# A linear attention and FP4 feed-forward block: Silu on ScalarE, tiles of two sequences, and x's rounding moved to VectorE

## The reference

```python
xn = layernorm(x)
# attention: 16 heads of 16 values, buckets of 64 tokens
q = softmax(q over the head's 16 values) * 0.25;  k = exp(k)
context[n] = sum over all buckets before n of  k_bucket^T v_bucket     # and the sums of k
attn = (q @ context) / max(q @ ksum, 1e-6);  branch1 = attn @ W_out.T
# feed-forward with fp4 quantise-dequantise of every operand, in blocks of 16
h = silu(fp4(xn) @ fp4(w_gate).T) * (fp4(xn) @ fp4(w_up).T)             # 704 wide
branch2 = fp4(h) @ fp4(w_down).T
out = x + branch1 + branch2
```

## Time and profile before

| | before |
|---|---|
| median of three runs | 1790.64 us (1788.91 to 1790.73) |
| the profiled execution's own time | 1790.21 us |
| its span, first to last instruction | 1788.5 us |
| DVE busy | 1723.7 us (96%) |
| PE busy | 1677.6 us (94%) |
| ACT busy | 1142.6 us (64%) |
| POOL busy | 599.4 us (34%) |
| DMA | 21 GB/s, 6.7% of 16 engines |

### The profile page before, as it was taken

One profiled execution on the slowest core, in us unless ns is written; L12 is line 12 of the kernel. 1 busy time (PEld: TensorE's weight loads), 2 busy tenths in 40 slices (PEclk: granted clock), 3 DMA queues, 4 the chain that ended last, 5 costly groups with the idle time before them and its releaser, 6 DMA issues.

```text
span 1788.5 us, 47623 instructions
## 1 busy us (share of the span) xinstructions
PE 1677.6 (94%) x12366; PEld 1147.8 (64%) x12366; DVE 1723.7 (96%) x4655; ACT 1142.6 (64%) x2840; POOL 599.4 (34%) x1053
## 2 busy tenths in 40 slices
PE   0289999999999999999999999999999999999997
PEld 0256666666666666666666666666666666666665
DVE  6769999999999999999999999999999999999997
ACT  2756666666666666666666666666666666666663
POOL 2723232333333333333333333333333333333330
PEclk9889999999999999999999999999999999999998
DMA  3000000000000000000000000000000000000000
GB/s 101 1 0 13 23 23 18 18 23 23 12 23 23 12 23 23 21 14 23 23 12 23 23 17 18 23 23 12 23 23 12 23 23 23 12 23 23 12 12 19
DMA packets 35849, 37.01 MB, mean 21 GB/s; under 512 B 2118, under 2 KB 35142, under 8 KB 35654
## 3 DMA queue, kind: packets, MB, share of 16 engines
q1 hardware_dynamic: 35830, 36.77, 6.7%
HBM read 19.99 MB, written 16.78 MB: 21 GB/s over the span
## 4 chain that ended last, share of the span: by engine, by line
DVE 44%; issue 32%; PE 11%; ACT 6%; DVEq 4%; POOL 2%; DMA 1%; ACTq 1%; SPq 0%; POOLq 0%
DVE hq_s L832 7%; DVE dmx L707 4%; DVE ga L727 4%; DVE hv L798 3%; DVE qmax L671 3%; DVE h L737 2%; DVE xq_s L845 2%; DVE drec L711 1%; ACT hqt L552 1%; ACT th L542 1%; DVE qsh L680 1%; DVE osum L868 1%; DVE xq_s L843 1%; ACT qexp L484 1%; DVE dz L703 1%
## 5 line engine op out<-in xcount | busy, mean ns | idle before, releaser
L348 POOL TENSOR_TENSOR xnt<-xnt 128x256 f16<-128x256 f32 x128 | 118.7, 928 | 728.1 <-ACT xnt L466 728.1
L552 ACT ACTIVATE hqt<-trp 128x512 f16<-128x512 f16 (+1 forms) x384 | 213.5, 556 | 183.1 <-PE trp L1108 180.8
L1127 PE MATMUL outp<-w_down_cat,hqt 128*128 128x256 f16 x1408 | 247.3, 274 | 0.0
L525 ACT ACTIVATE hm<-hv 128x704 bf16<-128x704 f32 x128 | 101.0, 789 | 153.9 <-DVE hv L798 153.9
L744 DVE TENSOR_REDUCE hblk<-h 128x44 f32<-128x704 f32 x128 | 183.9, 1436 | 0.1
L1050 PE MATMUL ctxp<-vaug,kexp 64*128 64x136 f32 x996 | 181.4, 302 | 0.0
L1041 PE MATMUL nump<-snap,qt 128*64 128x144 f32 x1024 | 180.8, 299 | 0.4 <-DVE snap L691 0.4
L502 ACT ACTIVATE att_t<-trp 128x256 f32<-128x256 f32 x128 | 49.2, 384 | 194.9 <-PE trp L1062 194.8
L1050 PEld LDWEIGHTS ctxp<-vaug,kexp 64*128 64x128 f32 x996 | 131.2, 186 | 49.5 <-issue 49.1
L339 POOL TENSOR_TENSOR att_t<-att_t 128x256 f16<-128x256 f32 x128 | 86.2, 673 | 218.1 <-ACT att_t L503 218.1
L355 POOL TENSOR_TENSOR xmid<-xmg,xv 128x256 f32<-128x256 f32 x128 | 117.0, 914 | 108.3 <-ACT xmg L517 108.3
(11 more groups left out here) (219 smaller groups left out, 5157.5 us busy)
## 6 DMA issues: line engine op xcount, KB each, us to landing
xring<-x SPq DMA_DIRECT2D x64, 256.0 KB, 2.7
out<-xring SPq DMA_DIRECT2D x64, 256.0 KB, 2.2
raw_qkv<-wqkv_t SPq DMA_DIRECT2D x1, 768.0 KB, 13.6
raw_gate<-wgate SPq DMA_DIRECT2D x1, 704.0 KB
raw_up<-wup SPq DMA_DIRECT2D x1, 704.0 KB
raw_down<-wdown SPq DMA_DIRECT2D x1, 704.0 KB, 12.2
raw_out<-wout_t SPq DMA_DIRECT2D x1, 256.0 KB, 13.4
```

Source lines behind the costliest of these rows:

```text
L348: nc.gpsimd.tensor_tensor(xnt[:, par, 1, :], xnt32[:, par, :], xnt[:, par, 0, :], ALU.subtract)\
L552: nc.scalar.activation(hqt[:, par, m0:m1, :], tr16[:, 0:(m1 - m0) * P] .rearrange("p (m k) -> p m k", k=P), ACT.Copy).then_inc(hqt_done, 1)
L1127: nc.tensor.matmul(downp, hqt[:, par, m, :], w_down_cat[:, m, :], start=(m == 0), stop=False)
```

## The change

Three things change together.

**Silu on ACT.** `tanh_gate` becomes `silu_gate`, which gives silu(gate) itself; DVE's addition-and-product L727 goes, and one product by up remains for each half. The constants are rescaled (c_u in place of c_gu). In ACT's step the second half stands where `magic_x_add` stood, behind the waits of `normalise`.

**Tiles of two sequences.** A tile holds 64 tokens of one sequence (s = 0) and the 64 tokens at the same place of another (s = 1). There are still 128 tiles. One snapshot and one `bucket` serve both sequences in a step. The context of each sequence takes its own columns; nump's matmuls for s = 0 and s = 1 write different halves of the partitions, one behind the other, and ctxp's matmuls contract all 128 tokens with 64 output rows (f = 0, 1) each. V is written by ACT in two instructions of 64 partitions. Each load and store is two DMAs of half the size, and the second snapshot is gone from DVE's step. hq_s and hqt share the memory of q_rows.

**x's rounding.** POOL's `round_x` and ACT's `magic_x_add` go. DVE does the two steps as fused operations on xm, between `gate_h` half 0 and `row_factor`, and behind `scale_h`.

The diff, cut to its core:

```diff
-                nc.scalar.activation(vaug[:, par, :, 0:P], kv[:, D:2 * D].rearrange("p (g e) -> p g e", g=HG), ACT.Copy,
-                                     scale=2.0 ** -19).then_inc(kv_done, 1)
+                for s in range(2):
+                    rows = slice(s * BUCKET, (s + 1) * BUCKET)
+                    nc.scalar.activation(vaug[rows, par, :, :, s, 0:VW].rearrange("p g f e -> p (g f) e"),
+                                         kv[rows, D:2 * D].rearrange("p (o e) -> p o e", e=VW), ACT.Copy,
+                                         scale=2.0 ** -19).then_inc(kv_done, 1)
...
-                act.wait_ge(xq_mag, after(t, 2, 1))
-                nc.scalar.activation(xmg[:, :], xm[:, :], ACT.Identity, bias=mround[:, :]).then_inc(xq_mag, 1)
...
-                nc.scalar.activation(th[:, half, :], unit[(par + half) % 2][0][:, 0:FH], ACT.Tanh, scale=c_g[:, :])\
-                    .then_inc(tanh_done, 1)
+                nc.scalar.activation(sg[:, half, :], unit[(par + half) % 2][0][:, 0:FH], ACT.Silu, scale=c_g[:, :])\
+                    .then_inc(silu_done, 1)
...
-                tanh_gate(k, 0, par)
+                silu_gate(k, 0, par)
                 split_xnt(k + 2, par)
                 magic_x(k + 2)
                 copy_qt(k + 1, odd)
-                tanh_gate(k, 1, par)
                 normalise_waits(k + 3)
                 mean_waits(n, d + 4)
-                magic_x_add(k + 2)
+                silu_gate(k, 1, par)
...
+            def snapshot(t):
+                dve.wait_ge(ctx_done, 1 + after(t - 1))
+                sums = ctxp[:, 0:2 * HG * CW].rearrange("p (i o c) -> p i o c", o=1, c=CW).broadcast_to([P, 2 * HG, 2, CW])
+                nc.vector.tensor_tensor(snap[:, :, :, :, 0:CW].rearrange("p g s f c -> p (g s) f c"), sums,
+                                        mask[:, :, :].rearrange("p (o f) c -> p o f c", o=1)
+                                        .broadcast_to([P, 2 * HG, 2, CW]), ALU.mult).then_inc(snap_done, 1)
...
-                nc.vector.scalar_tensor_tensor(ga[:, half, :], th[:, half, :], 1.0,
-                                               unit[(par + half) % 2][0][:, 0:FH], ALU.add, ALU.mult)\
-                    .then_inc(ga_done, 1)
-                nc.vector.tensor_tensor(h[:, par, half * FH:(half + 1) * FH], ga[:, half, :],
+                nc.vector.tensor_tensor(h[:, par, half * FH:(half + 1) * FH], sg[:, half, :],
                                         unit[(par + half) % 2][1][:, 0:FH], ALU.mult).then_inc(h_done, 1)
...
+            def round_x(t, part):
+                if part == 0:
+                    dve.wait_ge(xq_mag, after(t))
+                    dve.wait_ge(xq_step, after(t, 8, 6))
+                    nc.vector.scalar_tensor_tensor(xmid[:, :], xm[:, :], MROUND, xv[:, :], ALU.add, ALU.subtract)\
+                        .then_inc(xq_round, 1)
+                else:
+                    dve.wait_ge(xq_round, after(t, 2, 1))
+                    nc.vector.scalar_tensor_tensor(xq[:, :], xm[:, :], MROUND, xmid[:, :], ALU.add, ALU.subtract)\
+                        .then_inc(xq_round, 1)
...
-                snapshot(k, 1)
                 max_q(k + 1, odd)
...
                 gate_h(k, 0, par)
+                round_x(k + 2, 0)
                 row_factor(k - 1, odd)
-                times_up(k, 0, par)
                 attention(k, par, 0)
                 scale_h(k - 1, odd, 0)
                 scale_h(k - 1, odd, 1)
+                round_x(k + 2, 1)
                 attention(k, par, 1)
-                snapshot(k + 1, 0)
+                snapshot(k + 1)
                 attention(k, par, 2)
                 gate_h(k, 1, par)
                 attention(k, par, 3)
-                times_up(k, 1, par)
...
                 for g in range(HG):
+                    for s in range(2):
+                        rows = slice(s * BUCKET, (s + 1) * BUCKET)
+                        last = nc.tensor.matmul(nump[rows, g * 2 * SW:(g + 1) * 2 * SW],
+                                                qt[:, par, g * P + s * BUCKET:g * P + (s + 1) * BUCKET],
+                                                snap[:, g, s, :, :].rearrange("p f c -> p (f c)"), start=True, stop=True)
...
+                    for f in range(2):
+                        last = nc.tensor.matmul(ctxp[f * VW:(f + 1) * VW, g * 2 * CW:(g + 1) * 2 * CW],
+                                                kexp[:, par, g * P + f * VW:g * P + (f + 1) * VW],
+                                                vaug[:, par, g, f, :, :].rearrange("p s c -> p (s c)"),
+                                                start=False, stop=False, skip_group_check=True)
...
-                bucket(k, 0, par, False)
+                bucket(k, par, ends)
                 gate_up(k, 0, par, (0,))
                 transpose_h(k - 2, par, 1)
                 gate_up(k, 0, par, (1,))
                 transpose_h(k - 2, par, 2)
-                bucket(k, 1, par, ends)
                 gate_up(k, 1, par, (0,))
```

More of the change, by code:

```diff
@@ L258, in _ @@
                 sp.dma_start(dst[:, :, :], src).then_inc(done, 16)
[L260 to L271, removed]
+            SP_N = SEQ_TILES // 2
@@ L273, in _ @@
             for n in range(XCH):
-                load(n)
+                load(0, n)
                 if n >= STORE_LAG:
[L276 to L282, removed]
+                    store(0, n - STORE_LAG)
+            with sp.Fori(XCH, SP_N) as n:
+                load(0, n)
+                store(0, n - STORE_LAG)
@@ L285, in _ @@
+            with sp.Fori(1, NT // SEQ_TILES) as q:
+                for n in range(STORE_LAG):
+                    load(q, n)
+                    store(q - 1, SP_N - STORE_LAG + n)
+                with sp.Fori(STORE_LAG, SP_N) as n:
+                    load(q, n)
+                    store(q, n - STORE_LAG)
+            for n in range(SP_N - STORE_LAG, SP_N):
+                store(NT // SEQ_TILES - 1, n)
+            sp.wait_ge(x_out, NP * 32)
         @block.gpsimd
@@ L534, in copy_xqt, with silu_gate @@
                     .then_inc(xqt_done, 1)
-            def tanh_gate(t, half, par):
+            def silu_gate(t, half, par):
                 if not is_tile(t):
@@ L1040, in bucket @@
                 for g in range(HG):
-                    last = nc.tensor.matmul(nump[rows, g * SW:(g + 1) * SW],
-                                            qt[:, par, g * P + b * BUCKET:g * P + (b + 1) * BUCKET],
-                                            snap[:, b, g, :], start=True, stop=True)
+                    for s in range(2):
+                        rows = slice(s * BUCKET, (s + 1) * BUCKET)
+                        last = nc.tensor.matmul(nump[rows, g * 2 * SW:(g + 1) * 2 * SW],
+                                                qt[:, par, g * P + s * BUCKET:g * P + (s + 1) * BUCKET],
+                                                snap[:, g, s, :, :].rearrange("p f c -> p (f c)"), start=True, stop=True)
                 last.then_inc(num_done, 1)
@@ L1047, in bucket @@
                     return
-                pe.wait_ge(kv_done, after(t, 2))
+                pe.wait_ge(kv_done, after(t, 3))
                 for g in range(HG):
-                    last = nc.tensor.matmul(ctxp[:, g * CW:(g + 1) * CW], kexp[rows, par, g * P:(g + 1) * P],
-                                            vaug[rows, par, g, :], start=False, stop=False, skip_group_check=True)
+                    for f in range(2):
[3 more added lines that the diff above has]
+                                                start=False, stop=False, skip_group_check=True)
                 last.then_inc(ctx_done, 1)
```

154 lines of the change are left out of this document (75 added, 79 removed).

## The result

The kernel after takes 1840.38 us (median of four runs, 1839.93 to 1843.47) against 1790.0 us before: a ratio of 1.0287 [1.0271, 1.0303], slower. The prediction said 1832 us and slower with a chance of 0.53. The profiled execution took 1843.5 us, its span is 1841.8.

A forecast was written before the change was run, and what follows sets the result against it. It took ACT and PE, with two table loads a step, as the bound: accounts of 13.1 to 13.8 us gave a pace of 13.4 against 13.07, so 1790.2 + 128 x 0.33 = 1832 us, range 1652 to 1888.

The forecast's parts named there:

- Silu's table: On ACT, Silu was taken to have its own function table, bringing two loads a step, some 256 in all.
- Both rivals with a shared table: Silu shares Exp's table, no loads: PE bound, 1724 to 1743 us, chance 0.20; or matmuls overlap, 1640 to 1665, chance 0.18.
- loads at double price: Rival: each table load on ACT costs twice its row because the engine runs empty around it; 2127 us, chance 0.07.
- loads that count less: Rival: loads come, but c is near 1.3 or part of the load lies beside a wait; 1768 to 1788 us, chance 0.05.
- the case with overlap: Rival: shared table and the bucket's matmuls overlap, so PE drops below DVE's 12.0; 1650 us, chance 0.18.
- A load at its row's price: Each ACT table load costs about 1.28 us, as the profile's row of 1283 ns; pace 13.05 to 13.9, chance 0.50.
- The ring account: Loop through ACT and PE between transposes of the attention output: 13.18 less 2.63 idle plus two loads, 13.4 with V's second instruction.
- The PE account: PE's work per step, 12.55 - c, plus 1.28 us of load ahead of the gate: 13.83 - c, or 13.3.
- c: PE's gain per step from bucket neighbours writing different halves of the partitions: taken as 0.5 us, bounds 0 and 1.3.
- DVE's 12.0: DVE's work was to fall from 13.10 to 12.0 us a step.
- The blocking by POOL: POOL's two rounding steps hold up DVE's second scale_h product and dmx; moving them saves 0.55 and 0.44 us a step.
- PE waits for xnt: Sign: PE waits about 1.3 us in each step for xnt before the transposes of q.

The follow-up runs named there:

- experiment 1: Kernel after with Tanh called in Silu's place and DVE's addition left out, so the output lacks the product (tanh + 1) * gate: 1654.02 us.
- Experiment 10: Kernel after with all context matmuls written to one half of the partitions, the second sequence's attention and half of the context left out: 1862.65 us.
- experiment 4: Kernel before with x's two rounding steps moved from POOL to DVE, ACT's xmg gone and the second Tanh in its place: 1761.02 us.
- 7: Kernel before with tiles of two sequences alone, keeping Tanh and x's rounding on POOL: 1781.14 us.
- 5: Kernel after with a one-element Exp added ahead of split_att, so that Exp's table loads while ACT is idle: 1777.39 us.
- 8: Kernel after with the second of V's two instructions, and so the second sequence's V, left out: 1777.03 us.
- both cuts together: Kernel after with a one-element Exp ahead of split_att and the second sequence's V left out: 1776.0 us.
- the next repair: Kernel after with early one-element Exp, second V left out, and DVE's first half of h and xmid moved behind scale_h's two products: 1741.01 us.
- experiment 11: Kernel after with early one-element Exp, plus qmax and qsh ahead of hv on DVE, qexp and a one-element Silu ahead of hm on ACT: 1856.27 us.

## Why the prediction was right, by its own steps

**Silu's table: right.** 253 loads, no Silu among Exp's functions. Both rivals with a shared table (0.38 together) fell, and so did loads at double price and loads that count less; experiment 1 shows what a shared table would have given: 1654 us, where 1650 was named for the case with overlap.

**A load at its row's price: right in the main.** 1.43 a step, not 1.28 and not twice that, by the starts of kexp. The Trainium skill (ScalarE: Activation LUTs, What ACT_TABLE_LOAD costs) gives 1283 ns, which is the mean of the loads here, and a drain of 1380 ns besides; the start of kexp moved by 1.43 us with the load, so no such drain is to be seen.

**The ring account: right in its mechanism, with errors that nearly cancelled.** It read 13.18 - 2.63 + 2 x 1.28 + 0.32 = 13.43. Measured, the loads are 2.86, not 2.56. V's two instructions take 0.79 where the one had its whole 0.40 ahead of the gap: 0.39, not 0.32. Not counted was the overlap at hm, which starts 0.11 before hqt's copy has ended (910.87 against 910.98), while behind a gap it started after; nor that PE's stretch fell by 0.15. So 13.18 - 2.63 + 2.86 + 0.39 - 0.11 - 0.15 = 13.54, and the ring is 13.53. The forecast of 1832 us is closer to the measured 1840 than its pace was, and that is luck: by the prediction's sum a pace of 13.53 gives 1849 us. Of the 9 us between, 3 are the profiled execution, which took that much more than the median. Another 3 lie before the first bucket, which starts at 96.9 us and not at 99.9, and 2 behind the last one, from which the end is 30.1 us away and was 31.9.

**The PE account: not what binds.** It gave 13.83 - c with c = 0.5. Experiment 10 puts the overlap at 0.95, inside the bounds of 0 and 1.3; the merging of two stops and the 64 columns gave another 2.58 - 2.06 = 0.52 (two buckets of 1.29 in the kernel before, 907.11 to 908.40), where 0.32 was taken. PE works 83.74% of 13.53, 11.3 us. That these terms were too small by 0.65 cost the forecast nothing, because the ring of ACT and PE was the longer one and the bucket lies beside ACT's work in it. Had nothing overlapped, the pace would have been 13.67, by experiment 10. The Trainium skill (TensorE: Matmul & The Clock Gate, Part 3) says that matmuls in different column groups run concurrently, and experiment 10 agrees: 2.06 us against 1.11. The c near 1.3 that was worked out by its three-fold case didn't come.

**DVE's 12.0: right.** Experiment 1 runs at 12.03 with DVE fully busy. Scale_h's second product fell to its twin, dmx to 0.08 and so below the 0.18 that was taken, and xq cost 0.34 and the snapshot 0.64, as said. xmid, for which 0.1 to 0.2 more was allowed beside POOL's xnt split, took 0.46 us in experiment 1 (the median of its 128) and 0.60 to 0.68 in the kernel after, beside POOL's split (0.68 at 915.27, with the split from 915.00 to 915.67). The blocking by POOL was shown by experiments 4 and 7: it goes with POOL's two steps and comes back with them.

**PE waits for xnt: right** in place and size (1.48 against 1.3). Removing 0.5 of it elsewhere (5, 8) left that wait at 1.4 to 1.5 a step, and the time fell: how long a wait is doesn't say what a repair elsewhere in its ring is worth.

**What was missed** are the second ring, of ACT and DVE at 13.02, and the third, of PE and ACT through the bucket at 12.72. They changed nothing in the forecast, but the second is why the moved load alone, and both cuts together, stop at 1776 to 1777 us, 0.5 a step below the first ring, and the third is why the next repair stopped at 1741.

## What to carry to other kernels

Before a function on ScalarE is exchanged, find out whether it shares its table with the others of the loop: here one saved operation on VectorE, twice a step and worth 0.64 us together, was paid with two loads of 1.43 us on an engine that had looked one third idle. An engine's idle share is not room if its work lies in a ring; add up the ring from one instruction to itself in the next step, and look for the next ring close behind, since two repairs that each give 0.5 us may give 0.5 together. Changes that come in one patch should be timed one by one: here two of the three parts were good (1734 us together) and the third hid it.

## What the runs showed of the hardware

- Silu is not in the function table that Exp, Tanh and Square share: with Silu in the loop there are 253 loads in the steps, with Tanh none. A load of 1.28 us took 1.43 us of ACT's time. Square and Copy ran behind Silu without a load.
- Matmuls that write different halves of the output partitions run side by side: 16 instructions in 1.11 us, and 2.06 when all write the same half. The order in which they are issued made no difference (1.16).
- Two DVE instructions of 704 and 16 elements ran 0.55 us longer each beside POOL's steps on x; moving those steps to DVE made the kernel faster by 1.6% (experiment 4).
- In the kernel of experiment 11, PE's granted clock was 0.50, the 1.2 GHz level, from 904.30 to 907 us, right behind a wait of 1.86 us for ACT, and 1.00 from 917 to 921 us, where PE waits 1.70 us for ACT; in the kernel after, with waits of 1.5 us, it was 1.00 over the window at 950 us. What makes the difference isn't shown. Over 900 to 1000 us experiment 11 shows 0.98, so this is rare and not what makes its 13.6 a step. The windows of experiment 11 (columns as in the earlier trace rows):

```profile
904.30:907.00 2.70, 2.70 (x11) 1.80 (x12) 2.70 (x7) 1.32 (x4) 0.84 (x1) 0.50 0.00 0
917.00:921.00 4.00, 2.33 (x19) 1.68 (x20) 2.64 (x5) 3.47 (x10) 1.02 (x1) 1.00 0.00 0
```
